# A hybrid block on one Trainium2 core: residual additions moved from GpSimd to VectorE, four down tiles kept open in PSUM, and the last output rows prepared in another order

## The chip, the cores and the metric

The kernel runs on 1 core of one Trainium2 chip. The metric is the device time of one execution in microseconds (us), as the median of several runs. The names of the engines in the rows are PE (TensorE, matrix products; PEld is its weight load), DVE (VectorE), ACT (ScalarE), POOL (GpSimd) and SP (SyncE, which here only issues DMA transfers). A matrix product reads SBUF and writes PSUM, which has 8 banks of 128 x 512 float32 here.

## The reference

The block takes x of 4 batches x 512 tokens x 512 features, runs a gated delta-rule attention on its modulated layer norm, and then a feed-forward part of hidden width 2048:

```
h = _layernorm(x) * (1 + ca) + sa
x = x + ga * attention(h)
h = _layernorm(x) * (1 + cb) + sb
x = x + gb * ffn(h)         # ffn: (silu(h @ Wgate.T) * (h @ Wup.T)) @ Wdown.T
```

The change touches only the last line: the multiplication by the gate gb, the residual addition of x, and the store of the result.

## The kernel before

**The feed-forward part.** It runs as 16 iterations (function `iteration`, L1011). Iterations 0 to 7 treat batches 0 and 1, iterations 8 to 15 batches 2 and 3; each iteration takes one eighth of the hidden width. Every float32 factor is split into a high and a low part, so that a product is three matrix products. An iteration has 22 groups of six matrix products of 512 columns on PE: seven for the gate half (`prod(n, 0..6)` with n = 2 it), seven for the up half (n = 2 it + 1), and between them the eight *down* tiles of the iteration before. The seven products of a half are a Strassen-like scheme for four 128 x 512 blocks; `copy_s` (ACT, out of PSUM) and `cadd` (DVE) combine them. `silu` (ACT), `gated` (DVE), `fh` (ACT) and `fl` (DVE) then make the high and low part (FH, FL) of four blocks of silu(gate) * up.

**A down tile.** `down(it, k)` is one output tile of 128 tokens x 512 features: tile k belongs to the first batch of the two for k = 0 to 3, to the second for k = 4 to 7. PE writes it into one of two PSUM banks, 6 and 7 in turn (`ring_bank`, L890), and waits until DVE has taken the tile before last out of the bank (semaphore `v_y`). DVE adds the tile to its running sum YA[k] in SBUF (L2566).

**The weights.** Each iteration needs gate, up and down weights. For each, SP loads them, POOL forms the sums of the scheme (`w_comb`, L2683 to L2689), ACT makes the high part (`w_high`, one 128 x 1792 copy), and POOL the low part (`w_low_ff`, L2696, seven instructions; `w_high_d`, L2704, four instructions for the down weights). The first product of a half waits for its low part.

**The end of batches 0 and 1.** After the eighth down tile DVE multiplies YA[k] by the gate (`post_0`, into YA[k]). POOL then adds the residual x, which SP has loaded into X1[k] (`add_0`, L2732, eight instructions in iteration 8), and SP stores X1[k] (`store_0`).

**The end of batches 2 and 3.** For the last tiles the work is split: once YA[k] holds the sum of iterations 8 to 14, POOL forms YA[k] * gb + x (`out_pre`, L2739 and L2742; x lies in XO[k]). For `down(15, k)` DVE multiplies the PSUM tile by gb into XO[k] and adds it to YA[k], and SP stores YA[k] (L1458). XO[0] to XO[5] are loaded at iteration 10, XO[6] and XO[7] in iteration 15, since they overlie the gate weights (L1445). XO[0] to XO[3] count on one semaphore (`d_x2`), XO[4] to XO[7] on another (`d_x3`), and `out_pre` waits for all four of its batch:

```
                e.wait_ge(sem(f"d_x{2 + k // 4}"), 80 + 64)
```

In the last iteration `out_pre(0)` stands ahead of the up weights' low part on POOL.

**What sets the order.** One list of steps (`plan`) is written out by hand through calls of `step`. Each engine walks through it, takes the steps it knows and issues its instructions in that order. An instruction that waits for a semaphore holds up all that stand behind it on its engine, SP's DMA issues among them.

Of the kernel before, what the change touches and what calls it, by code (L numbers as in the profile page):

```python
# [53 lines left out]
def build(nc, x, W1, cw, dtb, alog, nw, Wo, cT, wmod, wgu, wdn, cst, out):  # L54
# [956 lines left out]
    def iteration(it):  # L1011
# [111 lines left out]
        cadd(n, 1)  # L1123
        if it and not last:
            down(it - 1, 7)
        if turn:
# [139 lines left out]
    def sync(e):  # L1266
# [21 lines left out]
        for st in plan:  # L1288
# [152 lines left out]
            elif kind == "store_0":  # L1441
                k = st["k"]
                e.wait_ge(sem("p_out"), k + 1)
                e.dma_start(out[k // 4, k % 4 * 128:k % 4 * 128 + 128, :], X1[k][:, :]).then_inc(sem("d_out"), 16)
            elif kind == "load_xo":  # L1445
# [732 lines left out]
    def vector(e):  # L2178
# [16 lines left out]
        for st in plan:  # L2195
# [357 lines left out]
            elif kind == "down":  # L2553
# [3 lines left out]
                if it % 8 == 0:  # L2557
                    if it:
                        e.wait_ge(sem("p_out"), k + 1)
# [4 lines left out]
                elif it < 15:  # L2564
                    e.wait_ge(sem("v_y"), 8 * (it - 1) + k + 1)
                    tt(y, bank(st["bank"]), y, ALU.add).then_inc(sem("v_y"), 1)  # L2566
                else:
                    e.wait_ge(sem("p_out"), 8 + 2 * k + 2)
                    tt(XO[k][:, :], bank(st["bank"]), gbB[k // 4][:, :], ALU.mult).then_inc(sem("v_y"), 1)
                    e.wait_ge(sem("v_y"), 8 * it + k + 1)  # L2570
                    tt(y, y, XO[k][:, :], ALU.add).then_inc(sem("out_x"), 1)
# [7 lines left out]
    def gpsimd(e):  # L2579
# [11 lines left out]
        for st in plan:  # L2591
# [125 lines left out]
            elif kind == "split_h" and st["on"] == "p":  # L2717
# [9 lines left out]
            elif kind == "add_0":
                k = st["k"]
                e.wait_ge(sem("v_om"), k + 1)
                e.wait_ge(sem(f"d_x{k % 2}"), (160, 144)[k % 2])  # L2730
                in_order()
                signal(e.tensor_tensor(X1[k][:, :], YA[k][:, :], X1[k][:, :], ALU.add), "p_out")  # L2732
# [85 lines left out]
```

## Time and profile before

| | |
|---|---|
| Median of 3 runs | 1050.65 us (1048.23 to 1051.37) |
| The profiled execution, its own time | 1049.25 us |
| Span of its trace | 1047.3 us |
| Busy share PE, DVE, ACT, POOL | 95%, 66%, 48%, 53% |

The span runs from the first to the last record of the trace; the execution's own time is 1.95 us longer. All positions below are in us from the start of the span. Iteration 9 begins near 805, iteration 10 near 842 and iteration 15 near 993. In the rows, L1464 is the helper for every matrix product, L1862 that for every ACT instruction, L2180 that for DVE's two-input instructions; POOL's lines tell the steps apart. A row "x30" merges 30 instructions in a row; some matrix-product records are missing from the trace, so counts are not exact. PEclk is the granted clock of TensorE, 1.00 for 2.4 GHz and 0.50 for 1.2 GHz.

### The profile page before, as it was taken

Reading aid. Unit: us, or ns where it says so; the run is one execution under the profiler, and the core shown is the slowest. Engines: PE = TensorE matmul, PEld = TensorE weight load, DVE = VectorE, ACT = ScalarE, POOL = GpSimd, SP = SyncE. Lnnn points to the kernel's source line nnn. Section 1 sums busy time; section 2 is a strip of 40 time slices with the busy share of each in tenths; the row PEclk is TensorE's granted clock in tenths of the full one; section 3 lists DMA queues with packets and bytes.
Section 4 is the critical chain, followed back from the end, with each engine's and each line's share of the span. In section 5 each row is a group of like instructions: output and inputs, shape, how many; then the busy total and the mean of one; then the engine's idle time right before and its main releaser. Section 6 shows DMA issues by size and latency. Waiting matters only on the chain.

```text
span 1047.3 us, 20631 instructions
## 1 busy us (share of the span) xinstructions
PE 996.5 (95%) x7920; PEld 787.9 (75%) x7920; DVE 688.9 (66%) x1044; ACT 501.2 (48%) x891; POOL 555.9 (53%) x597
## 2 busy tenths in 40 slices
PE   7999999999998999999799999999989899999997
PEld 4676777878677888888577777888867688878875
DVE  5977377899964777877763455555577455555447
ACT  3676575345545444554555644334453244434340
POOL 1222530022025554658566555877788866657675
PEclk9999999999998999999999999999999999999999
DMA  6504336938356566656242111111131232111112
GB/s 217 201 11 123 76 82 166 261 101 207 78 127 172 117 136 143 158 122 150 77 141 81 41 42 60 40 61 44 58 118 61 104 121 61 41 61 41 41 41 80
DMA packets 158209, 106.35 MB, mean 102 GB/s; under 512 B 93984, under 2 KB 131104, under 8 KB 157984
## 3 DMA queue, kind: packets, MB, share of 16 engines
q1 hardware_dynamic: 158112, 105.04, 35.9%
q8 instruction: 63, 1.03, 0.4%
q14 instruction: 34, 0.28, 0.1%
HBM read 75.65 MB, written 29.36 MB: 100 GB/s over the span
## 4 chain that ended last, share of the span: by engine, by line
PE 61%; POOL 11%; DVE 11%; ACT 5%; issue 5%; DMA 4%; SPq 2%; POOLq 0%; DVEq 0%; ACTq 0%
PE ps L1464 58%; ACT t L1862 5%; POOL t L2696 4%; DVE t L2180 3%; PE ps L1472 3%; DVE t L2290 2%; DMA scrU<-t 2%; SPq L1325 1%; POOL t L2732 1%; DVE t L2278 1%; PE ps L1703 1%; POOL t L2704 1%; POOL t L2725 1%; DVE t L2390 1%; DVE t L2190 1%
## 5 line engine op out<-in xcount | busy, mean ns | idle before, releaser
L1464 PE MATMUL ps<-t,t 128*128 128x512 f32 (+7 forms) x7100 | 942.5, 326 | 45.1 <-ACT t L1862 13.3
L1464 PEld LDWEIGHTS ps<-t,t 128*128 128x128 f32 (+4 forms) x7100 | 734.6, 160 | 238.2 <-issue 46.3
L2180 DVE TENSOR_TENSOR t<-ps,t 128x512 f32<-128x512 f32 (+2 forms) x336 | 234.3, 707 | 228.6 <-PE ps L1464 156.0
L1862 ACT ACTIVATE t<-t 128x512 fp32r<-128x512 f32 (+11 forms) x433 | 271.3, 650 | 220.8 <-DVE t L2180 95.5
L1862 ACT ACTIVATE t<-ps 128x512 f32<-128x512 f32 (+5 forms) x250 | 138.2, 560 | 244.0 <-PE ps L1464 226.4
L2180 DVE TENSOR_TENSOR t<-t,t 128x512 fp32r<-128x512 f32 (+15 forms) x249 | 208.8, 859 | 44.3 <-ACT t L1862 34.4
L2696 POOL TENSOR_TENSOR t<-t,t 128x256 fp32r<-128x256 f32 x217 | 160.7, 776 | 100.7 <-ACT t L1862 100.1
L1862 ACT ACTIVATE t<-ps,t 128x64 f32<-128x64 f32 (+3 forms) x157 | 74.3, 534 | 25.5 <-PE ps L1472 12.3
L2290 DVE SCALAR_TENSOR_TENSOR t<-ps,t,t 128x511 f32<-128x511 f32 (+2 forms) x108 | 80.2, 747 | 3.4 <-ACT t L1862 0.5
L2704 POOL TENSOR_TENSOR t<-t,t 128x256 fp32r<-128x256 f32 x64 | 63.6, 1024 | 17.3 <-ACT t L1862 15.9
L2627 POOL MEMSET t<- 128x3072 f32 x4 | 10.7, 2668 | 92.5 <-PE ps L1464 70.0
L1472 PE MATMUL ps<-t,t 128*128 128x128 f32 (+1 forms) x340 | 53.7, 288 | 1.6 <-DVE t L2185 1.3
L2671 POOL TENSOR_TENSOR t<-t,t 128x768 fp32r<-128x768 f32 x16 | 29.3, 1830 | 33.5 <-ACT t L1862 33.3
L1472 PEld LDWEIGHTS ps<-t,t 128*128 128x128 f32 (+1 forms) x340 | 39.0, 148 | 10.6 <-issue 5.4
L2608 POOL TENSOR_TENSOR t<-t,t 128x384 fp32r<-128x384 f32 x16 | 14.6, 915 | 52.6 <-PE ps L1464 32.7
L2597 POOL TENSOR_TENSOR t<-t,t 128x512 fp32r<-128x512 f32 x13 | 17.4, 1338 | 46.9 <-ACT t L1862 45.8
L2677 POOL TENSOR_TENSOR t<-t,t 128x512 f32<-128x512 f32 x16 | 21.4, 1337 | 38.1 <-DVE t L2180 37.4
L2683 POOL TENSOR_TENSOR t<-t 128x256 f32<-128x256 f32 x32 | 27.1, 847 | 4.6
L1862 ACT ACTIVATE t<-t,t 128x1 f32<-128x1 f32 (+2 forms) x36 | 13.2, 367 | 33.5 <-DVE t L2192 30.5
L2687 POOL TENSOR_TENSOR t<-t 128x256 f32<-128x256 f32 x32 | 26.4, 825 | 2.5
L2190 DVE BATCH_NORM_STATS2 t<-t 128x6 f32<-128x512 f32 x32 | 21.9, 684 | 8.1 <-DMA t<-in_x 6.4
L2632 POOL MEMSET t<- 128x1536 f32 x1 | 1.4, 1381 | 47.3 <-PE ps L1464 47.3
(60 smaller groups left out, 405.5 us busy)
## 6 DMA issues: line engine op xcount, KB each, us to landing
t<-in_wgu SPq DMA_DIRECT2D x32, 512.0 KB, 3.5
scrU<-t SPq DMA_DIRECT2D x60, 256.0 KB, 3.1
t<-scrU SPq DMA_DIRECT2D x32, 288.0 KB, 4.7
t<-in_wdn SPq DMA_DIRECT2D x32, 256.0 KB, 2.8
t<-scrU SPq DMA_DIRECT2D x32, 192.0 KB, 3.4
t<-in_W SPq DMA_DIRECT2D x19, 256.0 KB, 2.9
t<-in_x SPq DMA_DIRECT2D x16, 256.0 KB, 4.1
t<-in_wmod SPq DMA_DIRECT2D x4, 1024.0 KB, 5.5
```

The lines of the kernel that those rows point to most:

```text
L1464: return e.matmul(o, l, r_, start=start, stop=stop, skip_group_check=True)
L1472: return e.transpose(o, i, idn)
L1862: return e.activation(o, i, f, **kw)
L2180: return e.tensor_tensor(o, a, b, op)
L2190: e.bn_stats(st6[:, slot_, :], src).then_inc(sem(name + "bn"), 1)
L2290: e.scalar_tensor_tensor(yy[:, d + 1:SEQ], p_[:, 0:SEQ - d - 1], cwt[:, j, 2 - d:3 - d], yy[:, d + 1:SEQ], ALU.mult, ALU.add).then_inc(sem ...
L2671: signal(e.tensor_tensor(OZl[:, :, :], OZ[:, :, :], OZh[:, :, :].bitcast(f32), ALU.subtract), "p_ozl")
L2677: signal(e.tensor_tensor(YB[u % 2][:, :], YB[u % 2][:, :], XB[u % 2][:, :], ALU.add), "p_x1")
L2683: signal(e.tensor_tensor(r_[:, 4, :], r_[:, 0, :], r_[:, 3, :], ALU.add), "p_ws")
L2687: signal(e.tensor_tensor(r_[:, 0, :], r_[:, 1, :], r_[:, 0, :], ALU.subtract), "p_ws")
L2696: t = e.tensor_tensor(WGl[m % 3][:, i, :], WR[st["slot"]][:, i, :], WGh[m % 3][:, i, :].bitcast(f32), ALU.subtract)
L2704: t = e.tensor_tensor(WDl[it // 15][:, n, q], WDr[n][:, q], WDh[it // 15][:, n, q].bitcast(f32), ALU.subtract)
```

## The change

1. `add_0` goes from POOL to DVE: k = 0 and 1 in iteration 8 behind `gated(8, 1)`, k = 2, 3 and 4 at the end of iteration 8, and k = 5, 6, 7 in iteration 9, each behind one down tile. The stores move to the end of iteration 9, ahead of the loads of XO[0] to XO[5] in SP's order.
2. In the last iteration the steps of `out_pre` stand in the order 4, 5, (up weights' low part), 0, 1, 2, 3, (down weights' low part), 6, 7.
3. The last four down tiles of iteration 14 (k = 4 to 7) become `down_begun`: they stay open in banks 0, 1, 2 and 6, and `down_last` of iteration 15 accumulates on them, so DVE no longer takes them out. `down_last(0..3)` use banks 7, 4, 5 and 3. `down_begun(4)` stands between products 4 and 5 of the last up half.

```diff
@@ the plan
-        if it == 14:
-            step("out_pre", k=k)
+    HELD = {4: 0, 5: 1, 6: 2, 7: 6}
+    LAST = {0: (7, lambda: ring_free[7]), 1: (4, lambda: [("v_c", 95)]), 2: (5, lambda: [("v_c", 96)]),
+            3: (3, lambda: [("v_gf", 63)])}
+    def down_begun(k):
+        free = ring_free[6] if HELD[k] == 6 else [("v_c", 93), ("a_si", 63)]
+        step("down_begun", k=k, bank=HELD[k], free=free)
@@ iteration, gate half
             if last:
                 w_high(up_m(it), [("prod", 7 * (n - 1) + 7)])
+                out_pre(4)
+                out_pre(5)
+                w_low_ff(up_m(it))
...
             down(it - 1, 0)
+            if last:
+                out_pre(0)
...
+            if last and k < 4:
+                out_pre(k)
+            if it == 9 and k < 4:
+                add_0(k + 4)
@@ iteration, up half
-        if it and not last:
+        if last:
+            down_begun(4)
+        elif it:
             down(it - 1, 7)
...
             if it == 8:
-                for k in range(8):
-                    step("add_0", k=k)
+                add_0(0, 1)
...
         if it == 8:
+            add_0(2, 3, 4)
+        if it == 9:
             for k in range(8):
                 step("store_0", k=k)
@@ the end
-    for k in range(4, 8):
-        down(14, k)
+    for k in range(5, 8):
+        down_begun(k)
+    for k in (6, 7):
+        out_pre(k, [("v_fl", 64)])
     for k in range(8):
-        down(15, k)
+        down_last(k)
@@ DVE
+            elif kind == "down_last":
+                k = st["k"]
+                e.wait_ge(sem("down"), 120 + k + 1)
+                e.wait_ge(sem("p_out"), out_at(k))
+                tt(XO[k][:, :], bank(st["bank"]), gbB[k // 4][:, :], ALU.mult).then_inc(sem("v_y"), 1)
+                e.wait_ge(sem("v_y"), 116 + k + 1)
+                tt(YA[k][:, :], YA[k][:, :], XO[k][:, :], ALU.add).then_inc(sem("out_x"), 1)
+            elif kind == "add_0":
+                k = st["k"]
+                e.wait_ge(sem("v_om"), k + 1)
+                e.wait_ge(sem(f"d_x{k % 2}"), (160, 144)[k % 2])
+                tt(X1[k][:, :], YA[k][:, :], X1[k][:, :], ALU.add).then_inc(sem("v_om"), 1)
@@ POOL, out_pre
-                e.wait_ge(sem("v_y"), 112 + k + 1)
-                if k == 0:
+                e.wait_ge(sem("v_y"), (104 if k > 3 else 112) + k + 1)
+                for tok in st["free"]:
+                    e.wait_ge(*at_least(tok))
+                if k == 4:
                     e.wait_ge(sem("a_grow"), 6)
```

POOL's instructions at the end, before. The tiles t_237 to t_244 are YA[0] to YA[7], t_257 to t_264 are XO[0] to XO[7], t_265 and t_266 the gates; t_185<-t_179 is the low part of the last up weights, t_189 that of the last down weights.

```order
L2739 TENSOR_TENSOR t_237<-t_237,t_265 128x512 [waits p_wl,a_grow,v_y]
L2742 TENSOR_TENSOR t_237<-t_237,t_257 128x512 [waits p_out,d_x2]
L2696 TENSOR_TENSOR t_185<-t_179,t_183 128x256 [waits p_out,a_wh]
L2696 TENSOR_TENSOR t_185<-t_179,t_183 128x256 x6
L2739 TENSOR_TENSOR t_238<-t_238,t_265 128x512 [waits p_wl,v_y]
L2742 TENSOR_TENSOR t_238<-t_238,t_258 128x512 [waits p_out,d_x2]
L2739 TENSOR_TENSOR t_239<-t_239,t_265 128x512 [waits p_out,v_y]
L2742 TENSOR_TENSOR t_239<-t_239,t_259 128x512 [waits p_out,d_x2]
...
L2739 TENSOR_TENSOR t_241<-t_241,t_266 128x512 [waits p_wl,v_y]
L2742 TENSOR_TENSOR t_241<-t_241,t_261 128x512 [waits p_out,d_x3]
```

The same place of the changed kernel:

```order
L2803 TENSOR_TENSOR t_241<-t_241,t_266 128x512 [waits p_wl,a_grow,v_y]
L2806 TENSOR_TENSOR t_241<-t_241,t_261 128x512 [waits p_out,d_x3]
L2803 TENSOR_TENSOR t_242<-t_242,t_266 128x512 [waits p_out,v_y]
L2806 TENSOR_TENSOR t_242<-t_242,t_262 128x512 [waits p_out,d_x3]
L2764 TENSOR_TENSOR t_185<-t_179,t_183 128x256 [waits p_out,a_wh]
L2764 TENSOR_TENSOR t_185<-t_179,t_183 128x256 x6
L2803 TENSOR_TENSOR t_237<-t_237,t_265 128x512 [waits p_wl,v_y]
L2806 TENSOR_TENSOR t_237<-t_237,t_257 128x512 [waits p_out,d_x2]
...
L2803 TENSOR_TENSOR t_243<-t_243,t_266 128x512 [waits p_wl,v_fl,v_y]
L2806 TENSOR_TENSOR t_243<-t_243,t_263 128x512 [waits p_out,d_x3]
```

Two tiles now stand ahead of the low part of the up weights instead of one, and they are tiles 4 and 5, whose addition waits for `d_x3`; tiles 0 to 3 follow it, and tiles 6 and 7 stand behind the down weights.

DVE at the end of iteration 8, before, from `gated(8, 1)` (t_216<-t_232) to `cadd(18, 0)` (t_213<-ps,t_210). The rows t_217<-ps and t_218<-t_234 are `gated(8, 2)` and `gated(8, 3)`, and t_226, t_227, t_228 the `fl` of the last three blocks:

```order
L2180 TENSOR_TENSOR t_216<-t_232,t_216 128x512 [waits v_c,a_si]
L2180 TENSOR_TENSOR t_217<-ps,t_217 128x512 [waits prod,a_si]
L2180 TENSOR_TENSOR t_234<-ps,t_211 128x512 [waits down,prod,a_sp]
L2180 TENSOR_TENSOR t_218<-t_234,t_218 128x512 [waits v_c,a_si]
L2180 TENSOR_TENSOR t_226<-t_216,t_220 128x512 [waits a_fh]
L2180 TENSOR_TENSOR t_227<-t_217,t_221 128x512 [waits a_fh]
L2180 TENSOR_TENSOR t_228<-t_218,t_222 128x512 [waits a_fh]
L2180 TENSOR_TENSOR t_213<-ps,t_210 128x512 [waits v_fl,prod,a_sp]
L2180 TENSOR_TENSOR t_214<-ps,t_212 128x512 [waits v_fl,prod,a_sp]
L2563 COPY t_237<-ps 128x512 [waits p_out,down]
```

The same place of the changed kernel, up to the last `fl`; t_249 to t_253 are X1[0] to X1[4]:

```order
L2241 TENSOR_TENSOR t_216<-t_232,t_216 128x512 [waits v_c,a_si]
L2241 TENSOR_TENSOR t_249<-t_237,t_249 128x512 [waits d_x0,v_om]
L2241 TENSOR_TENSOR t_250<-t_238,t_250 128x512 [waits d_x1,v_om]
L2241 TENSOR_TENSOR t_217<-ps,t_217 128x512 [waits prod,a_si]
L2241 TENSOR_TENSOR t_234<-ps,t_211 128x512 [waits down,prod,a_sp]
L2241 TENSOR_TENSOR t_218<-t_234,t_218 128x512 [waits v_c,a_si]
L2241 TENSOR_TENSOR t_226<-t_216,t_220 128x512 [waits a_fh]
L2241 TENSOR_TENSOR t_227<-t_217,t_221 128x512 [waits a_fh]
L2241 TENSOR_TENSOR t_251<-t_239,t_251 128x512 [waits d_x0,v_om]
L2241 TENSOR_TENSOR t_252<-t_240,t_252 128x512 [waits d_x1,v_om]
L2241 TENSOR_TENSOR t_253<-t_241,t_253 128x512 [waits d_x0,v_om]
L2241 TENSOR_TENSOR t_228<-t_218,t_222 128x512 [waits a_fh]
```

Two additions now stand ahead of `gated(8, 2)` and three ahead of the last `fl` and `cadd(18, 0)`.

PE in the last up half, before: t_201 and t_202 begin products 5 and 6, and t_186<-t_222 a down tile of iteration 14. Only the rows that begin or end a group are shown.

```order
L1464 MATMUL ps<-t_207,t_183 128x512 x2
L1464 MATMUL ps<-t_201,t_183 128x512 [waits a_sp]
...
L1464 MATMUL ps<-t_208,t_183 128x512 x2
L1464 MATMUL ps<-t_202,t_183 128x512 [waits v_c]
...
L1464 MATMUL ps<-t_209,t_183 128x512 x2
L1464 MATMUL ps<-t_186,t_222 128x512 [waits v_fl,v_y]
...
L1464 MATMUL ps<-t_186,t_222 128x512 [waits v_y]
```

The same place of the changed kernel:

```order
L1505 MATMUL ps<-t_207,t_183 128x512 x2
L1505 MATMUL ps<-t_186,t_222 128x512 [waits v_fl,a_si,v_c]
...
L1505 MATMUL ps<-t_187,t_220 128x512
L1505 MATMUL ps<-t_201,t_183 128x512 [waits a_sp]
...
L1505 MATMUL ps<-t_208,t_183 128x512 x2
L1505 MATMUL ps<-t_202,t_183 128x512 [waits v_c]
...
L1505 MATMUL ps<-t_209,t_183 128x512 x2
L1505 MATMUL ps<-t_186,t_222 128x512 [waits a_si,v_c]
```

One down tile has moved ahead of product 5, and these tiles wait for `a_si` and `v_c`, no longer for `v_y`, which DVE counts up when it takes a tile out.

## Rows read from the trace of the kernel before

**Rows 1.** Timeline of PE, 775 to 900: start, us, instructions, [idle before <-releaser]
```profile
...
814.87 11.25 PE L1464 MATMUL ps<-t,t 128*128 128x512 f32 x48 [1.33 <-ACT t L1862]
826.62 3.03 PE L1464 MATMUL ps<-t,t 128*128 128x512 f32 x12 [0.50 <-POOL t L2696]
832.21 68.16 PE L1464 MATMUL ps<-t,t 128*128 128x512 f32 x290 [2.56 <-ACT t L1862]
```

**Rows 2.** Timeline of POOL, 775 to 900
```profile
...
805.85 3.28 POOL L2704 TENSOR_TENSOR t<-t,t 128x256 fp32r<-128x256 f32 x4 [0.43 <-POOL t L2689]
...
821.67 4.90 POOL L2696 TENSOR_TENSOR t<-t,t 128x256 fp32r<-128x256 f32 x7
```

**Rows 3.** Line L2732: ns min/median/max, first and last start
```profile
...
L2732 POOL TENSOR_TENSOR t<-t,t x8: 1287/1298/1529, 809.3 to 820.2; 128x512 f32<-128x512 f32 x8
```

**Rows 4.** Timeline of ACT, 775 to 900
```profile
...
806.00 1.23 ACT L1862 ACTIVATE t<-t 128x512 fp32r<-128x512 f32 x2 [2.55 <-DVE t L2180]
...
814.24 0.58 ACT L1862 ACTIVATE t<-ps 128x512 f32<-128x512 f32 x1
814.72 2.21 ACT L1862 ACTIVATE t<-t 128x1792 fp32r<-128x1792 f32 x2
...
829.98 1.70 ACT L1862 ACTIVATE t<-t 128x1792 fp32r<-128x1792 f32 x1 [10.62 <-POOL t L2689]
```

**Rows 5.** Timeline of DVE, 775 to 900
```profile
...
807.27 5.79 DVE L2180 TENSOR_TENSOR t<-t,t 128x512 f32<-128x512 f32 x4
812.99 0.68 DVE L2180 TENSOR_TENSOR t<-ps,t 128x512 f32<-128x512 f32 x1
...
873.40 3.27 DVE L2180 TENSOR_TENSOR t<-t,t 128x512 f32<-128x512 f32 x4
```

**Rows 6.** Timeline of SP's DMA issues, 775 to 900
```profile
...
845.68 2.76 SPq L1453 DMA_DIRECT2D t<-scrX  x6
856.39 10.89 SPq L1418 DMA_DIRECT2D t<-in_wgu  x2
```

**Rows 7.** Stretches: us, busy of the five, PEclk, DMA share, GB/s
```profile
...
832.20:837.00 4.80, 4.79 (x14) 3.83 (x15) 2.61 (x3) 1.11 (x2) 4.80 (x7) 0.64 0.01 3
...
1010.80:1012.50 1.70, 0.00 (x1) 0.00 (x0) 0.69 (x1) 0.00 (x0) 1.66 (x3) 1.00 0.00 0
```

**Rows 8.** Timeline of PE, 985 to the end
```profile
...
1012.51 7.10 PE L1464 MATMUL ps<-t,t 128*128 128x512 f32 x30 [1.71 <-POOL t L2696]
1020.29 5.78 PE L1464 MATMUL ps<-t,t 128*128 128x512 f32 x24 [0.69 <-ACT t L1862]
1027.86 15.30 PE L1464 MATMUL ps<-t,t 128*128 128x512 f32 x60 [1.79 <-DVE t L2180]
```

**Rows 9.** Timeline of POOL, 985 to the end
```profile
...
994.29 3.85 POOL L2704 TENSOR_TENSOR t<-t,t 128x256 fp32r<-128x256 f32 x4 [0.30 <-ACT t L1862]
1004.72 1.29 POOL L2739 TENSOR_TENSOR t<-t,t 128x512 f32<-128x512 f32 x1 [6.59 <-DVE t L2180]
...
1007.60 4.86 POOL L2696 TENSOR_TENSOR t<-t,t 128x256 fp32r<-128x256 f32 x7
...
1038.74 1.55 POOL L2742 TENSOR_TENSOR t<-t,t 128x512 f32<-128x512 f32 x1
```

**Rows 10.** Timeline of SP's DMA issues, 985 to the end
```profile
...
1006.71 0.80 SPq L1453 DMA_DIRECT2D t<-scrX  x2
```

**Rows 11.** DMA issues, 985 to the end: count, KB each, median us to landing
```profile
...
t<-scrX SPq DMA_DIRECT2D x2, 256.0 KB, 2.8
```

**Rows 12.** Timeline of DVE, 985 to the end
```profile
...
1009.48 0.69 DVE L2180 TENSOR_TENSOR t<-ps,t 128x512 f32<-128x512 f32 x1 [0.68 <-PE ps L1464]
1010.84 0.69 DVE L2180 TENSOR_TENSOR t<-ps,t 128x512 f32<-128x512 f32 x1 [0.67 <-PE ps L1464]
...
1038.08 1.06 DVE L2180 TENSOR_TENSOR t<-t,t 128x512 f32<-128x512 f32 x1
...
1040.76 0.68 DVE L2180 TENSOR_TENSOR t<-ps,t 128x512 f32<-128x512 f32 x1
```

More of the change, by code:

```diff
@@ L901, in down, with out_pre, out_at, add_0 @@
             step("post_0", k=k)
-        if it == 14:
-            step("out_pre", k=k)
+    out_order = []
+    def out_pre(k, free=()):
+        step("out_pre", k=k, free=list(free))
+        out_order.append(k)
+    def out_at(k):
+        return 2 * out_order.index(k) + 2
+    def add_0(*ks):
+        for k in ks:
+            step("add_0", k=k)
+    HELD = {4: 0, 5: 1, 6: 2, 7: 6}
[4 more added lines that the diff above has]
+        step("down_begun", k=k, bank=HELD[k], free=free)
+        tick("down")
+    def down_last(k):
+        i, free = (HELD[k], lambda: []) if k in HELD else LAST[k]
+        step("down_last", k=k, bank=i, free=free(), begun=k in HELD)
+        tick("down")
+        tick("v_y")
     def gate_row(b):
@@ L1066, in iteration @@
             step("silu", it=it, t=1)
-            w_load_next(it, w_low_ff(up_m(it)))
+            if not last:
+                w_load_next(it, w_low_ff(up_m(it)))
             prod(n, 5)
@@ L1442, in sync @@
                 k = st["k"]
-                e.wait_ge(sem("p_out"), k + 1)
+                e.wait_ge(sem("v_om"), 8 + k + 1)
                 e.dma_start(out[k // 4, k % 4 * 128:k % 4 * 128 + 128, :], X1[k][:, :]).then_inc(sem("d_out"), 16)
@@ L1454, in sync @@
                         sem(f"d_x{2 + k // 4}"), 16)
-            elif kind == "down" and st["it"] == 15:
+            elif kind == "down_last":
                 k = st["k"]
@@ L1857, in tensor @@
                     t = mm3(bank(st["bank"]), FH[f][:, tk], FL[f][:, tk], WDh[it // 15][:, jj, :], WDl[it // 15][:, jj, :], jj == 0, jj == 1)
+                t.then_inc(sem("down"), 1)
+            elif kind in ("down_begun", "down_last"):
+                k = st["k"]
+                b, s = k // 4, k % 4
+                tk = slice(s * 128, (s + 1) * 128)
+                ahead = kind == "down_begun"
+                it = 14 if ahead else 15
+                for tok in st["free"]:
+                    e.wait_ge(*at_least(tok))
+                if ahead and k == 4:
+                    e.wait_ge(sem("v_fl"), 60)
+                elif not ahead and s == 0:
+                    e.wait_ge(sem("v_fl"), 64 if b else 63)
+                if not ahead and k == 0:
+                    e.wait_ge(*at_least(w_low_at[47]))
+                opens = ahead or not st["begun"]
+                for jj, t_ in enumerate(((0, 2), (3, 1))[b]):
+                    f = f_of(it, t_)
+                    t = mm3(bank(st["bank"]), FH[f][:, tk], FL[f][:, tk], WDh[it // 15][:, jj, :], WDl[it // 15][:, jj, :],
+                            opens and jj == 0, not ahead and jj == 1)
                 t.then_inc(sem("down"), 1)
@@ L2558, in vector @@
                     if it:
-                        e.wait_ge(sem("p_out"), k + 1)
+                        e.wait_ge(sem("v_om"), 8 + k + 1)
                     else:
@@ L2563, in vector @@
                     e.tensor_copy(y, bank(st["bank"])).then_inc(sem("v_y"), 1)
-                elif it < 15:
+                else:
                     e.wait_ge(sem("v_y"), 8 * (it - 1) + k + 1)
                     tt(y, bank(st["bank"]), y, ALU.add).then_inc(sem("v_y"), 1)
[L2567 to L2571, printed above, removed]
+            elif kind == "down_last":
+                k = st["k"]
[5 more added lines that the diff above has]
+            elif kind == "add_0":
+                k = st["k"]
+                e.wait_ge(sem("v_om"), k + 1)
+                e.wait_ge(sem(f"d_x{k % 2}"), (160, 144)[k % 2])
+                tt(X1[k][:, :], YA[k][:, :], X1[k][:, :], ALU.add).then_inc(sem("v_om"), 1)
             elif kind == "post_0":
@@ L2726, in gpsimd @@
                 signal(t, "p_hs")
[L2727 to L2732, printed above, removed]
             elif kind == "out_pre":
                 k = st["k"]
-                e.wait_ge(sem("v_y"), 112 + k + 1)
-                if k == 0:
+                e.wait_ge(sem("v_y"), (104 if k > 3 else 112) + k + 1)
+                for tok in st["free"]:
+                    e.wait_ge(*at_least(tok))
+                if k == 4:
                     e.wait_ge(sem("a_grow"), 6)
```

## The prediction

> **What bounds the kernel now.** I read the timelines of the five engines beside each other at the two places that the change touches, and at each place asked which wait ends last.
>
> From 775 to 900, PE's timeline shows three waits in iteration 9: 1.33 us before 814.87, for ACT; 0.50 us before 826.62, for POOL's low part of the up weights; and 2.56 us before 832.21, for ACT again. After that it runs to 900 without a gap [rows 1]. POOL's timeline explains the second: the low part of the down weights ends at 809.13, and the low part of the up weights, seven instructions, only starts at 821.67 and ends at 826.57 [rows 2]. The eight additions lie between, 1.29 to 1.53 us each [rows 3], 12.5 us in all with their gaps. The third follows from the same backlog: the weight copy at 829.98, 1.70 us long, came when POOL's sums were done, and a PSUM copy that PE wants stands behind it on ACT; ACT had idled 10.62 us for it [rows 4]. The first wait has to do with DVE. Four of its SBUF instructions took 5.79 us beside POOL's additions, and `cadd(18, 0)` came only at 812.99; the same four take 3.27 us in iteration 10 [rows 5]. `silu(9, 0)` waits for that `cadd`, the copy at 814.24 stands behind it on ACT [rows 4], and PE waits for the copy. The stores and loads behind the additions are in SP's order [rows 6].
>
> The waits have a second price, the clock. After the 2.56 us gap the granted clock was 0.64 over the next 4.80 us, so it had fallen to 1.2 GHz for most of them; that is 4.80 x 0.36 = 1.7 us of work lost. Over the 1.70 us gap at 1010.80 it stayed at 1.00, 2.4 GHz [rows 7].
>
> At the end, PE waits 1.71 us for POOL before 1012.51, 0.69 us for ACT before 1020.29, and 1.79 us for DVE before 1027.86; the last ten groups take 15.30 us [rows 8]. POOL idles 6.59 us before its first `out_pre` at 1004.72, which then stands ahead of the low part at 1007.60 [rows 9]. SP issues the loads of XO[6] and XO[7] at 1006.71, when the gate products are through [rows 10]; such a load lands in 2.8 us [rows 11]. A down tile takes PE 1.36 us, as DVE's evictions at 1009.48 and 1010.84 show [rows 12].
>
> **The change part by part: iterations 8 and 9.** Without the additions POOL's low part can start when ACT's weight copy is done: 814.72 + 1.70 [rows 4] = 816.4 instead of 821.67, 5.2 us earlier, and what hangs on it comes earlier by as much. PE wanted it 0.50 us earlier, and the copy behind it 2.56 us earlier, so both waits go, with the slow clock behind them: 0.50 + 2.56 + 1.7 = 4.8 us.
>
> Against that, DVE gets eight instructions. Two stand ahead of `gated(8, 2)`. They run beside POOL's down weights, so I take 1.06 us each, which an addition takes beside POOL [rows 12]: 2.1 us. ACT's `fh(8, 2)`, the second instruction at 806.00 [rows 4], waits for it, and the copy that PE needs behind it, so a wait of about 2 us appears earlier. The next three run while POOL now idles: 0.69 us each, 2.1 us. The four at 807.27 shrink from 5.79 to 4 x 0.7 = 2.8 us. So `cadd(18, 0)` comes 2.1 + 2.1 - 3.0 = 1.2 us later; as SBUF instructions overlap by up to 0.1 us each, I take 0.8. The three in iteration 9 each stand between two evictions: 0.69 + 1.06 = 1.75 us against PE's 1.36, three times 0.4, less the 0.67 that DVE has free, is 0.5 us. The five additions cost nothing further while ACT and the second bank hide them. The gain here is 4.8 - 0.8 - 0.5 = 3.5 us. Bounds: 4.8 if all is hidden; 0.7 by the first rival below.
>
> The page SBUF: State Buffer of the Trainium skill (two separate sides) says that a DVE instruction with two SBUF inputs and a GpSimd instruction that reads SBUF exclude each other for a whole instruction. By that rule each of the first two additions could wait out one low-part instruction, 3.28 / 4 = 0.82 us, and last 1.5 us instead of 1.06, which would make the gain 2.6 us. That additions took 1.45 us each beside POOL's 512-wide ones and 1.06 at the end speaks for a wait of less than a whole instruction on average.
>
> SP: eight stores now lie ahead of the loads at 845.68, at 2.76 / 6 = 0.46 us each 3.7 us, then a landing of some 3 us, for which the loads wait, then their 2.8 us. That is 9.5 us of the 10.7 until the next weight load at 856.39 [rows 6]. Hidden; if not, 2 us of lateness meet some 10 us before the weights are used.
>
> **The end.** Here a new wait arises. POOL's second instruction for tile 4 waits for `d_x3`, and that count holds all of XO[4] to XO[7]. XO[6] and XO[7] are issued at 1006.71; the second leaves 0.4 us later and lands 2.8 us later, at 1009.9. In before, POOL had other work until then. Now the multiplication of tile 4 fits into POOL's idle time after 998.1, and then POOL stands still, with the up weights' low part queued behind it and PE waiting for that. Then come three instructions of 1.44 us (1.29 and the gap), 4.3 us, and 4.86 us of low part: 1019.1. PE starts the up half 6.6 us later than at 1012.51.
>
> PE then loses fewer waits: 0.69 (a down tile stands in it), 1.79 (no eviction is needed), 15.30 - 10 x 1.36 = 1.7 and 5.78 - 4 x 1.36 = 0.3 us [rows 8]: 4.5 us. The count of groups is unchanged. POOL's next work, eight instructions of tiles 0 to 3 at about 1.5 us and 3 to 3.9 us of down weights [rows 9], ends by 1035.1. PE comes to the first last tile at 1019.1 + 7.1 + 6 x 1.36 = 1034.4, or 1036.1 with the slow clock: no wait then, 0.7 us if the clock held.
>
> PE idles from 1010.8 to 1019.1, 8.3 us, three times the gap after which the clock fell [rows 7]. I charge the same 1.7 us. The page TensorE: Matmul & The Clock Gate of the Trainium skill (Part 1) says that an idle array is granted half rate; its rule would not change this term.
>
> DVE's last part: tiles 6 and 7 on POOL run until about 1042, and beside POOL a tile costs DVE 1.70 us, against 1.33 later and PE's 1.36. Some three tiles times 0.34 less a little regained is 0.8 us at the end. The stretch from DVE's last instruction to the end of the span is unchanged.
>
> End: 6.6 - 4.5 + 1.7 + 0.8 = +4.6 us. Bounds: +2.8 with neither clock nor lag; +7 with the slow clock twice as long and a later landing.
>
> **Sum.** +4.6 - 3.5 = +1.1 us. It is made against the profiled execution: 1047.3 becomes 1048.4 us of span, and its own time of 1049.25 becomes 1050.35. The median of the runs is 1.4 us above that execution, so 1051.7 us.
>
> **The rivals.** *Slower:* the gap in iteration 8 slows the clock. It grows from 1.33 us to more than 2; 1.71 did not cost the clock and 2.56 did. If the three additions ahead of the last `fl` also take 1.06 us, 1.1 us more, the gap passes 2.5 us, and the clock takes 1.7 us. The gain is 3.5 - 2.8 = 0.7, the time 1050.65 + 3.9 = 1054.5 us. For it speaks how near the numbers lie; against it, that the wait falls into two pieces and that POOL idles there. It decides from 2.5 us in one piece on. *Slower at the end:* the 8.3 us gap leaves a longer stretch of slow clock, or the loads land later, by 2 us together: 1053.7 us. *Faster:* POOL is not held by `d_x3`, because the loads are in time. Then PE's 1.71 us go too, and the end gains 1.7 + 4.5 - 0.8 = 5.4 us, with the 3.5 before: 1041.8 us. Against it stands that the loads wait for products that end at 1006.7, 8 us after POOL is ready. *The stores on SP* delay the weights: against it the margin above; a lateness of 3 us on PE would make 1054.7 us.
>
> **How the numbers follow.** Forecast 0.60, first rival 0.20, second 0.08, the faster one 0.07, the stores 0.05. A measurement of this kernel tells about 0.3%, 3.15 us, from no change: 1047.5 to 1053.8 us. The forecast's own spread is 1048.3 (4.8 gained, 2.8 - 0.3 lost) to 1054. A sixth of it (0.10) passes 1053.8 and a fifteenth (0.04) falls under 1047.5; of the first rival 0.15, of the second 0.04 and of the stores 0.04 pass 1053.8. That makes 0.11 faster with the third rival, 0.33 slower, and 0.56 within. The range for 8 in 10 reaches from 1048.0 to 1056.0 us, to the slower cases and without the faster one.
>
> **What would show it.** Right: in iteration 9 no PE wait for POOL, the clock at 1.00 from 826 to 840, PE waits of 2 to 2.5 us in all between 805 and 817; at the end a POOL wait of about 10 us for a DMA, PE idle about 8 us for the up weights' low part, a clock of 0.5 after it, and no PE wait for DVE in the last 14 us. Wrong: POOL's instruction of tile 4 before 1004; a PE gap of over 2.5 us near 810 to 816 with the clock down; the up weights of iteration 11 late because of SP.

## The result, and the profile after

| | before | changed |
|---|---|---|
| median of 20 runs | 1048.8 us (1046.3 to 1053.0) | 1051.2 us (1047.5 to 1056.9) |
| ratio | | 1.0024, 95% interval 1.0013 to 1.0035 |
| span of the profiled execution | 1047.3 us | 1048.3 us |

The changed kernel is 0.24% slower, 2.4 us by the medians. The spans differ by only 1.0 us, because the changed execution was already 1.2 us ahead before any changed code: PE's restart in iteration 8 lies at 780.29 instead of 781.46. So I count from places inside the program, and not from the start of the span.

PE's timeline of the changed kernel from 770 to 870. The waits of 0.50 and 2.56 us of [rows 1] are gone; one of 2.40 us has come at 808.90, where product 2 of half 18 waits for ACT's copy. After it PE runs without a gap.

```profile
...
795.21 11.29 PE L1505 MATMUL ps<-t,t 128*128 128x512 f32 x48 [0.45 <-ACT t L1923]
808.90 61.45 PE L1505 MATMUL ps<-t,t 128*128 128x512 f32 x261 [2.40 <-ACT t L1923]
```

POOL, same stretch: behind the down weights it now idles 8.71 us, and the low part of the up weights follows ACT's copy, where [rows 2] had it at 821.67 behind the additions.

```profile
...
804.66 3.71 POOL L2772 TENSOR_TENSOR t<-t,t 128x256 fp32r<-128x256 f32 x4 [0.43 <-POOL t L2757]
817.08 5.37 POOL L2764 TENSOR_TENSOR t<-t,t 128x256 fp32r<-128x256 f32 x7 [8.71 <-ACT t L1923]
```

ACT: the two `fh` that stood together at 806.00 [rows 4] are now 2.28 us apart, since the second waits for `gated(8, 2)`; the copy for PE stands behind it. The weight copy at 826.70 no longer holds anybody.

```profile
...
804.82 0.64 ACT L1923 ACTIVATE t<-t 128x512 fp32r<-128x512 f32 x1 [2.54 <-DVE t L2241]
807.73 0.63 ACT L1923 ACTIVATE t<-t 128x512 fp32r<-128x512 f32 x1 [2.28 <-DVE t L2241]
808.27 0.58 ACT L1923 ACTIVATE t<-ps 128x512 f32<-128x512 f32 x1
...
826.70 1.70 ACT L1923 ACTIVATE t<-t 128x1792 fp32r<-128x1792 f32 x1 [6.32 <-POOL t L2757]
```

DVE: four instructions with the first two additions, 4.62 us; then seven in 4.30 us, with three additions, while POOL idles, against 5.79 us for four in [rows 5]; `cadd(18, 0)` at 812.62. Of the three additions between evictions the first takes 0.88 us, the other two 0.68 each.

```profile
...
802.48 4.62 DVE L2241 TENSOR_TENSOR t<-t,t 128x512 f32<-128x512 f32 x4
...
808.40 4.30 DVE L2241 TENSOR_TENSOR t<-t,t 128x512 f32<-128x512 f32 x7
812.62 0.68 DVE L2241 TENSOR_TENSOR t<-ps,t 128x512 f32<-128x512 f32 x1
...
820.97 0.88 DVE L2241 TENSOR_TENSOR t<-t,t 128x512 f32<-128x512 f32 x1
...
822.37 0.68 DVE L2241 TENSOR_TENSOR t<-t,t 128x512 f32<-128x512 f32 x1
```

SP: the stores, the loads and the next weight load in [rows 6]'s place. The weights are issued at 853.63, right behind the loads, and 847.25 + 4.91 = 852.16 is when POOL freed their buffer: 1.5 us late, which shows on no engine.

```profile
...
842.76 5.43 SPq L1485 DMA_DIRECT2D out<-t  x8
850.88 2.71 SPq L1494 DMA_DIRECT2D t<-scrX  x6
853.63 9.44 SPq L1459 DMA_DIRECT2D t<-in_wgu  x2
```

The end. PE's timeline: one wait of 8.32 us for POOL's low part, and then no other, where [rows 8] has 1.71, 0.69 and 1.79.

```profile
...
1014.92 29.02 PE L1505 MATMUL ps<-t,t 128*128 128x512 f32 x114 [8.32 <-POOL t L2764]
```

POOL, against [rows 9]: the multiplication of tile 4 at 994.10, then 10.21 us of waiting for a DMA, two more instructions of tile 5, and only then the low part of the up weights (L2764) that PE waits for. The down weights' low part (L2772) ends at 1030.1, before PE needs it.

```profile
...
994.10 1.53 POOL L2803 TENSOR_TENSOR t<-t,t 128x512 f32<-128x512 f32 x1 [0.17 <-POOL t L2772]
1005.84 1.27 POOL L2806 TENSOR_TENSOR t<-t,t 128x512 f32<-128x512 f32 x1 [10.21 <-DMA t<-scrX]
...
1008.66 1.26 POOL L2806 TENSOR_TENSOR t<-t,t 128x512 f32<-128x512 f32 x1
1010.06 4.80 POOL L2764 TENSOR_TENSOR t<-t,t 128x256 fp32r<-128x256 f32 x7
...
1026.98 3.10 POOL L2772 TENSOR_TENSOR t<-t,t 128x256 fp32r<-128x256 f32 x4
...
1037.14 1.56 POOL L2806 TENSOR_TENSOR t<-t,t 128x512 f32<-128x512 f32 x1
```

SP issues the loads that POOL waits for at 1002.51 ([rows 10]: 1006.71, the same step):

```profile
...
1002.51 0.80 SPq L1494 DMA_DIRECT2D t<-scrX  x2
```

The granted clock (the columns are those of [rows 7]) behind both waits: 0.50 for 3 us behind the first. In the second it fell while PE still waited, and from PE's restart at 1014.92 on it stayed at 0.50 until some 0.4 us after 1020.

```profile
...
808.90:811.90 3.00, 3.00 (x7) 2.42 (x8) 3.00 (x6) 0.67 (x2) 0.00 (x0) 0.50 0.51 175
811.90:814.90 3.00, 3.00 (x14) 2.41 (x14) 1.41 (x3) 1.28 (x3) 0.00 (x0) 0.96 0.00 0
1010.00:1018.00 8.00, 3.08 (x7) 2.49 (x8) 0.00 (x0) 0.11 (x1) 7.51 (x10) 0.51 0.01 2
1018.00:1020.00 2.00, 2.00 (x6) 1.54 (x5) 0.00 (x0) 0.48 (x1) 1.86 (x2) 0.50 0.00 0
1020.00:1022.00 2.00, 2.00 (x9) 1.59 (x9) 1.40 (x2) 0.11 (x1) 1.83 (x2) 0.91 0.00 0
```

DVE's last instructions: a tile costs 1.70 us while POOL works on tiles 6 and 7, and 1.33 later; the last tile starts 0.54 us after PE's end at 1043.94, against 0.25 us in the kernel before.

```profile
...
1038.19 1.07 DVE L2241 TENSOR_TENSOR t<-t,t 128x512 f32<-128x512 f32 x1
...
1039.89 0.69 DVE L2241 TENSOR_TENSOR t<-t,t 128x512 f32<-128x512 f32 x1
...
1044.48 0.68 DVE L2241 TENSOR_TENSOR t<-ps,t 128x512 f32<-128x512 f32 x1
```

### The profile page after: what moved, and what is told of

It reads as the page before. It is cut to its first block, busy times and chain, and to the rows that moved or that the text cites. A ratio compares the mean times of both kernels' runs of the same rounds, so it can differ in the third digit from the quotient of the medians.

```text
span 1048.3 us, 20624 instructions
## 1 busy us (share of the span) xinstructions
PE 994.5 (95%) x7920; PEld 788.7 (75%) x7920; DVE 690.9 (66%) x1048; ACT 502.3 (48%) x891; POOL 546.9 (52%) x589
## 4 chain that ended last, share of the span: by engine, by line
PE 66%; DVE 10%; POOL 7%; ACT 5%; issue 4%; DMA 4%; SPq 3%; DVEq 0%; POOLq 0%; ACTq 0%
PE ps L1505 62%; ACT t L1923 4%; PE ps L1513 3%; DVE t L2241 3%; DVE t L2351 2%; POOL t L2764 2%; DMA scrU<-t 2%; SPq L1366 1%; DVE t L2339 1%; PE ps L1744 1%; POOL t L2793 1%; DVE t L2451 1%; DMA scrA<-t 1%; DVE t L2251 1%; DVE t L2462 1%
## 5 line engine op out<-in xcount | busy, mean ns | idle before, releaser
L1505 PE MATMUL ps<-t,t 128*128 128x512 f32 (+7 forms) x7100 | 941.0, 325 | 47.8 <-ACT t L1923 11.3
L2241 DVE TENSOR_TENSOR t<-ps,t 128x512 f32<-128x512 f32 (+2 forms) x332 | 231.1, 706 | 232.2 <-PE ps L1505 169.9
L2241 DVE TENSOR_TENSOR t<-t,t 128x512 fp32r<-128x512 f32 (+14 forms) x257 | 214.5, 856 | 43.3 <-ACT t L1923 33.1
L2764 POOL TENSOR_TENSOR t<-t,t 128x256 fp32r<-128x256 f32 x217 | 161.3, 778 | 107.5 <-ACT t L1923 107.1
L2772 POOL TENSOR_TENSOR t<-t,t 128x256 fp32r<-128x256 f32 x64 | 64.2, 1033 | 17.3 <-ACT t L1923 15.9
L2665 POOL TENSOR_TENSOR t<-t,t 128x512 fp32r<-128x512 f32 x13 | 17.4, 1340 | 46.8 <-ACT t L1923 45.7
L2751 POOL TENSOR_TENSOR t<-t 128x256 f32<-128x256 f32 x32 | 27.7, 864 | 4.6
L2755 POOL TENSOR_TENSOR t<-t 128x256 f32<-128x256 f32 x32 | 26.1, 817 | 2.5
L2757 POOL TENSOR_TENSOR t<-t 128x256 f32<-128x256 f32 x32 | 25.2, 788 | 2.5
```

The source lines that it names most:

```text
L1505: return e.matmul(o, l, r_, start=start, stop=stop, skip_group_check=True)
L2241: return e.tensor_tensor(o, a, b, op)
L2751: signal(e.tensor_tensor(r_[:, 4, :], r_[:, 0, :], r_[:, 3, :], ALU.add), "p_ws")
L2755: signal(e.tensor_tensor(r_[:, 0, :], r_[:, 1, :], r_[:, 0, :], ALU.subtract), "p_ws")
L2757: signal(e.tensor_tensor(r_[:, 6, :], r_[:, 2, :], r_[:, 5, :], ALU.subtract), "p_ws")
L2764: t = e.tensor_tensor(WGl[m % 3][:, i, :], WR[st["slot"]][:, i, :], WGh[m % 3][:, i, :].bitcast(f32), ALU.subtract)
```

## The experiments

All eight were timed beside the kernel before, e1 to e4 together and e5 to e8 together, and the changed kernel at another time. So a difference to the changed kernel is best read from the two ratios to the kernel before; by them e1 is 9.2 us below it, by the medians 10.0. As executions of one kernel spread by several us, I also read two stretches of each profiled execution: *A* from PE's restart in iteration 8 (781.46 in the kernel before) to SP's issue of XO[6] and XO[7] (1006.71), which holds all that the additions and stores can do; and *B* from there to the end of the span.

| kernel | median us | ratio to before (95%) | A | B |
|---|---|---|---|---|
| before | | 1 | 225.3 | 40.6 |
| changed | 1051.2 | 1.0024 (1.0013 to 1.0035) | 222.2 | 45.8 |
| e1, own count | 1041.2 | 0.9936 (0.9921 to 0.9952) | 222.4 | 36.1 |
| e2, additions only | 1046.6 | 0.9980 (0.9959 to 1.0000) | 220.9 | 41.6 |
| e3, end only | 1054.2 | 1.0065 (1.0047 to 1.0082) | 223.6 | 46.0 |
| e4, filled gap | 1050.3 | 1.0016 (1.0002 to 1.0030) | 222.3 | 45.4 |
| e5, both mended | 1037.8 | 0.9906 (0.9882 to 0.9930) | 219.3 | 36.0 |
| e6, held tiles alone | 1047.3 | 0.9983 (0.9971 to 0.9996) | 223.6 | 38.8 |
| e7, weights first | 1046.1 | 0.9960 (0.9946 to 0.9974) | 220.8 | 41.5 |
| e8, additions later | 1051.0 | 1.0015 (1.0002 to 1.0029) | 222.4 | 45.7 |

The kernel before had medians of 1048.6 us beside e1 to e4 and 1049.0 us beside e5 to e8.

**e1: is it the shared count?** The loads of XO[6] and XO[7] count on another semaphore, which only the first loads of the kernel use:

```diff
-                        sem(f"d_x{2 + k // 4}"), 16)
+                        sem("d_x4" if k > 5 else f"d_x{2 + k // 4}"), 16)
...
-                e.wait_ge(sem(f"d_x{2 + k // 4}"), 80 + 64)
+                e.wait_ge(*((sem("d_x4"), 80) if k > 5 else (sem(f"d_x{2 + k // 4}"), 80 + (32 if k > 3 else 64))))
```

> The changed kernel with one edit: the loads of XO[6] and XO[7] count on a semaphore of their own, and POOL's additions of tiles 4 and 5 wait only for XO[4] and XO[5], loaded in iteration 10. Theory (the shared count holds POOL, and the slow clock follows from PE's wait): POOL's addition of tile 4 comes right behind its multiplication, the low part of the up weights ends before PE has done its down tiles, PE starts the up half without a wait 8.3 us earlier, the clock stays at 1.00, which gives 2.7 us more; 11 us less than the changed kernel, about 1040 us. Rival (two tiles ahead of the weights are too much work for POOL, whatever they wait for): a PE wait of 1.5 us or more for the low part stays, and the time is 1043 us or more.

9 to 10 us less than the changed kernel, and B is 9.7 us shorter. PE's timeline has no wait at the up half any more; the one before the last eight tiles is 0.39 us:

```profile
...
810.32 213.05 PE L1505 MATMUL ps<-t,t 128*128 128x512 f32 x916 [2.44 <-ACT t L1923]
1023.76 11.30 PE L1505 MATMUL ps<-t,t 128*128 128x512 f32 x48 [0.39 <-DVE t L2241]
```

POOL does both tiles back to back, in what was idle time, and the low part (L2764) ends at 1006.9, 1.3 us before PE is done with its down tiles:

```profile
...
995.48 1.53 POOL L2803 TENSOR_TENSOR t<-t,t 128x512 f32<-128x512 f32 x1 [0.17 <-POOL t L2772]
997.15 1.57 POOL L2806 TENSOR_TENSOR t<-t,t 128x512 f32<-128x512 f32 x1
...
1002.01 4.92 POOL L2764 TENSOR_TENSOR t<-t,t 128x256 fp32r<-128x256 f32 x7
```

The rival falls: the two tiles fit. The expectation of 8.3 + 2.7 = 11 us was 1.3 too large for B; the 0.39 us are one part of that, and VectorE's last instruction ends 2.65 us after PE, against 1.95 in the changed kernel.

**e2: the additions alone.** The kernel before with part 1 of the change only.

> The kernel before with only the residual additions on VectorE and the stores at the end of iteration 9; the end as before. Theory: PE reaches the end of its first gate product of iteration 10 some 3.0 us earlier than in the kernel before, counted from its restart in iteration 8, and the time is 3 us less, 1045.8 us; a PE wait of 2.4 us for ACT with a clock below 1.00 behind it shows near 808. Rival (the wait and the clock take back all): 1048.8 us, within 0.5 us of before.

2.1 us less by the ratio, with no change just at the end of the interval, so the time does not decide between the two. The wait of 2.44 us is there, but this time the clock did not fall behind it, so A is 4.4 us shorter, not 3.0:

```profile
...
808.19:811.19 3.00, 3.00 (x13) 2.50 (x14) 3.00 (x6) 1.23 (x2) 0.00 (x0) 1.00 0.61 175
```

Instead it fell behind the 1.79 us wait at the end, which the kernel before has too ([rows 8]) without this loss; that makes B 1.0 us longer, although nothing was changed there:

```profile
...
1021.60:1025.00 3.40, 3.40 (x9) 2.68 (x10) 1.23 (x2) 0.00 (x0) 3.10 (x3) 0.56 0.00 0
```

**e3: the end alone.** The changed kernel with `add_0` on POOL in iteration 8 and the stores there.

> The changed kernel with the additions back on GpSimd in iteration 8 and the stores there: only the end is changed. Theory: the stretch from SP's loads of XO[6] and XO[7] to the end of the span is 45.8 us against 40.6 in the kernel before, and the time is 5.2 us more, 1054 us. Rival (the two places interact, since the end gets its clock or its order from earlier work): the time is within 2 us of before.

5.6 us more by the medians, and B is 46.0, as the theory has it; the rival falls. The two parts add up as well as such runs can tell: -1.9 and +5.6 us by the medians against +2.4 for both, with intervals of some 2 us on each side of the single ones. In A the clock held behind the 2.56 us wait that in the kernel before had cost it:

```profile
...
832.39:834.39 2.00, 2.00 (x9) 1.66 (x10) 1.41 (x2) 0.31 (x1) 2.00 (x3) 1.00 0.00 0
```

**e4: the clock by itself.** 32 matrix products in the gap, behind the third down tile, for whose result nobody asks:

```diff
             step("load_xo", ks=(6, 7))
+            step("keep")
...
+            elif kind == "keep":
+                e.wait_ge(sem("v_c"), 93)
+                e.wait_ge(sem("a_si"), 63)
+                for _ in range(32):
+                    mm(bank(0), FH[0][:, 0:128], WDh[0][:, 0, :], True, True)
```

> The changed kernel with 32 additional matrix products (their result goes to bank 0 and is overwritten) behind the third down tile of iteration 15, ahead of the product that waits for the up weights; they take some 7 us of PE's 8.3 us wait. It isolates the clock. Theory (the rest of the loss at the end is the clock): the wait for POOL ends at the same place, the clock is 1.00 behind it, and the time is 2.7 us less than the changed kernel, 1048.5 us. Rival (PE's groups behind the wait are slow for another reason, the semaphores or PSUM): the time stays at 1051.2 us although the clock is 1.00.

The clock stays at 1.00 and the time hardly moves: 0.8 us less than the changed kernel by the ratios, within their intervals. That is the rival's time, but not for its reason, since PE's groups behind the wait do get faster. PE comes to the last eight tiles 28.0 us after SP's issue, against 30.5 in the changed kernel (1043.94 - 8 x 1.36 - 1002.51), and loses most of these 2.5 us to a wait that did not exist in the changed kernel: 1.61 us for the low part of the down weights.

```profile
...
1017.82 15.38 PE L1506 MATMUL ps<-t,t 128*128 128x512 f32 x66 [1.24 <-POOL t L2770]
1034.81 11.32 PE L1506 MATMUL ps<-t,t 128*128 128x512 f32 x48 [1.61 <-POOL t L2778]
```

```profile
...
1008.57 1.29 POOL L2812 TENSOR_TENSOR t<-t,t 128x512 f32<-128x512 f32 x1 [10.22 <-DMA t<-scrX]
...
1028.78 1.30 POOL L2812 TENSOR_TENSOR t<-t,t 128x512 f32<-128x512 f32 x1
1030.22 4.45 POOL L2778 TENSOR_TENSOR t<-t,t 128x256 fp32r<-128x256 f32 x4
```

In the changed kernel POOL ends the down weights' low part 27.6 us after SP's issue, here 29.4 us after it (1034.67 - 1005.23), and had it kept to 27.6, PE, which comes at 28.0, would not have waited. 1.35 of these 1.9 us lie in the four instructions of the low part, 4.45 us against 3.10. They run beside four `fl` of DVE, which come 2.4 us earlier, counted from the issue, because PE is faster, and which take 4.12 us instead of 2.82:

```profile
...
1029.96 4.12 DVE L2247 TENSOR_TENSOR t<-t,t 128x512 f32<-128x512 f32 x4
```

So a faster PE makes DVE and POOL meet, and that costs most of what it gains; removing the slow clock alone is worth 0.4 us in B.

**e5: the additions off ACT's path as well.** e1, and the additions 0 and 1 behind `cadd(18, 0)`, 2 and 3 behind the first down tile, 4 to 7 behind down tiles 1 to 4 of iteration 9.

```diff
             cadd(n, 0)
+            if it == 9:
+                add_0(0, 1)
...
             down(it - 1, 0)
+            if it == 9:
+                add_0(2, 3)
...
-            if it == 9 and k < 4:
-                add_0(k + 4)
+            if it == 9 and k < 5:
+                add_0(k + 3)
...
             if it == 8:
-                add_0(0, 1)
+                pass
...
-        if it == 8:
-            add_0(2, 3, 4)
```

> The version with XO[6] and XO[7] counted apart, and the eight additions all in iteration 9: 0 and 1 behind the first cadd, 2 and 3 behind the first down tile, 4 to 7 behind down tiles 1 to 4. Theory (two additions ahead of gated(8, 2) hold ACT's copy and so PE, 2.4 us and the clock after it): the wait near 808 goes, no other of over 0.5 us comes, and the time is 2.4 to 3.7 us less than that version, 1038.2 us. Rival (VectorE has no room for eight additions in iteration 9 either): a wait of the same size appears between 812 and 828, and the time stays at 1041 us.

As expected: 1037.8 us, 0.94% under the kernel before, and the fastest of all. The wait at 808 and the clock behind it are gone; 0.39 us at 825.34 has come:

```profile
...
794.07 30.87 PE L1507 MATMUL ps<-t,t 128*128 128x512 f32 x132 [0.45 <-ACT t L1925]
825.34 192.37 PE L1507 MATMUL ps<-t,t 128*128 128x512 f32 x832 [0.39 <-ACT t L1925]
1018.10 11.34 PE L1507 MATMUL ps<-t,t 128*128 128x512 f32 x48 [0.39 <-DVE t L2243]
```

**e6: the held tiles alone.** The kernel before with `down_begun` and `down_last`, and `out_pre` in its old order 0 to 7.

> The kernel before with only the down tiles 4 to 7 of iteration 14 kept open and the banks and place of the last tiles as in the changed kernel; the additions on GpSimd in iteration 8 and the order of out_pre 0 to 7 as before. Theory (held tiles are worth 4.5 us less a lag of VectorE): the 1.71 us wait for the up weights stays, those of 0.69 and 1.79 us go, the last groups run dense, VectorE lags by up to 2 us beside POOL's last tiles; the stretch from the loads of XO[6] and XO[7] to the end is 38 us against 40.6 before, the time 1046.2 us. Rival (a held tile gains nothing, the end is bound by POOL and VectorE): 40 us or more, 1048.5 us.

1.8 us less by the ratio, between the theories. The 1.71 us wait stays, and those of 0.69 and 1.79 us became one of 1.01:

```profile
...
1010.62 15.39 PE L1498 MATMUL ps<-t,t 128*128 128x512 f32 x66 [1.71 <-POOL t L2752]
1027.03 11.33 PE L1498 MATMUL ps<-t,t 128*128 128x512 f32 x48 [1.01 <-issue]
```

The row names no releaser. By the kernel these products need the `fl`, the third of which ends at 1026.93, 0.1 us before PE goes on. DVE makes the `fl` beside POOL's tiles 4 and 5: four instructions in 5.85 us. In the changed kernel the same four take 2.82 us, since POOL only begins with tile 6 when the last `fl` is done.

```profile
...
1022.78 5.85 DVE L2234 TENSOR_TENSOR t<-t,t 128x512 f32<-128x512 f32 x4
```

```profile
...
1029.62 2.82 DVE L2241 TENSOR_TENSOR t<-t,t 128x512 f32<-128x512 f32 x4
```

**e7: the weights ahead of the two tiles.** The changed kernel with `w_low_ff(up_m(it))` ahead of `out_pre(4)` and `out_pre(5)`.

> The changed kernel with the low part of the up weights ahead of tiles 4 and 5 on POOL; the shared count stays. Theory: PE starts the up half without a wait, but POOL still stands still until the loads land, and then has eleven instructions of tiles 4, 5, 0 to 3 ahead of the down weights' low part; PE waits some 4 us for it before the last eight tiles; the stretch from the loads to the end is 40 us, the time 1045.4 us. Rival (only the place of the up weights matters): no wait of over 1 us, 36 us as in the version with a count of its own, 1041.2 us.

0.4% under the kernel before, 1046.1 us where 1045.4 was expected. PE starts the up half at once, and then waits 5.05 us for L2772, 1 us more than I had expected; its last eight tiles take 13.27 us instead of the 11.3 of e1, since the clock fell in that wait and was 0.50 for 4.3 us behind it. That makes B 41.5 instead of 40. A is 1.4 us shorter than in the changed kernel with the same code there: behind its 2.41 us wait the clock stayed at 1.00. The rival falls:

```profile
...
1026.83 13.27 PE L1505 MATMUL ps<-t,t 128*128 128x512 f32 x48 [5.05 <-POOL t L2772]
```

```profile
...
1003.04 1.30 POOL L2803 TENSOR_TENSOR t<-t,t 128x512 f32<-128x512 f32 x1 [0.17 <-POOL t L2764]
1005.90 1.29 POOL L2806 TENSOR_TENSOR t<-t,t 128x512 f32<-128x512 f32 x1 [1.56 <-DMA t<-scrX]
...
1023.21 3.48 POOL L2772 TENSOR_TENSOR t<-t,t 128x256 fp32r<-128x256 f32 x4
```

**e8: the first two additions behind the fl.** The changed kernel with `add_0(0, 1, 2, 3, 4)` at the end of iteration 8.

> The changed kernel with additions 0 and 1 moved behind the second and third fl of iteration 8, to the other three; five additions now stand ahead of the last fl and cadd(18, 0). Theory (the chain through cadd(18, 0), silu and ACT's copy is what ends last, and the additions lengthen it wherever they stand ahead of it): the wait near 808 goes and one of about 2.3 us comes before product 5 near 814; the time is that of the changed kernel, 1051.2 us. Rival (only the copy that PE waits for at 808 matters): no such wait, 2.4 us less, 1048.8 us.

The time is that of the changed kernel, and the rival falls. The wait at 808 has gone, and one of 2.13 us has come before product 5, at 816.14, again with the slow clock behind it:

```profile
...
796.85 17.16 PE L1505 MATMUL ps<-t,t 128*128 128x512 f32 x72 [0.46 <-ACT t L1923]
816.14 192.27 PE L1505 MATMUL ps<-t,t 128*128 128x512 f32 x826 [2.13 <-ACT t L1923]
```

```profile
...
816.14:819.14 3.00, 3.00 (x8) 2.38 (x9) 1.27 (x2) 2.34 (x3) 1.39 (x3) 0.55 0.00 0
```

## Why the prediction was right, and where its sizes were off

*Iterations 8 and 9.* Right: the two waits behind POOL's backlog go, SP's stores stay hidden, and `cadd(18, 0)` comes 0.8 us later, counted from product 2 of half 17 (796.41 before, 795.21 after): 16.58 us before, 17.41 after. e8 shows that it is this chain, and not only the `fh`, that ends last. I took 3.5 us of gain and A gives 3.0.

The term that was mis-sized is the clock, "1.7 us": I counted it as won, but it fell again behind the new wait, 3 us at 0.50, 1.6 us lost. I had that as the first rival, from 2.5 us in one piece on, and had put against it that the wait would fall into two pieces; it came as one of 2.40, and that was enough; my sign of being wrong, over 2.5 us with the clock down, stood 0.1 us away. The bound of 2.5 us was no bound: the clock fell behind 2.13 us in e8 and behind 1.79 us in e2, and held behind 2.56 us in e3 and e6. So the 1.7 us that I read in one execution of the kernel before are not in every execution; where the clock held on both sides, A goes from 223.6 (e3, e6) to 220.9 (e2), 2.7 us.

Other errors made up for most of the 1.6 us. The additions between evictions, which I had charged 0.5 us, cost nothing: they took 0.88, 0.68 and 0.68 us, where I had taken 1.06 each. PE's wait grew by 1.07 us (1.33 to 2.40) and not by 0.8. And 0.9 us more was gained than these terms explain: 3.5 - 1.6 + 0.5 - 0.3 + 0.9 = 3.0. When e3 and e2, whose clock held in both, are matched matrix product by matrix product, PE loses 1.5, 0.6 and 2.8 us at the three waits of [rows 1], 0.5 us more than the rows print in their brackets; where the rest lies is open.

The 1.45 us "beside POOL's 512-wide ones" in the prediction is a mean over two cases and over no addition: of the four instructions at 807.27 the first two ran beside the low part and took 1.25 and 1.22 us, the other two beside POOL's additions and took 1.78 and 1.77. The first pair was the one to take for the two additions ahead of `gated(8, 2)`, which run beside the low part as well: they took 1.24 and 1.23 us, more than my 1.06. By the rule of the page SBUF: State Buffer in the Trainium skill (two separate sides), one instruction waits out the other's, and I had worked out 1.5 us from it. The trace agrees that both sides pay: alone the additions take 0.68 us, and two of POOL's four low-part instructions took 1.17 and 1.19 us beside them instead of 0.74. But the additions waited some 0.55 us each, less than a whole instruction of POOL.

*The new wait.* Right to the place and nearly to the tenth. From SP's issue: POOL's addition of tile 4 starts 3.33 us later (I had 3.2), PE starts the up half 12.41 us later against 5.80, 6.6 us more (6.6), after 8.32 us of idleness (8.3). e1 shows the cause, since it changes only what is counted.

*What PE recovers.* From its start to its end PE takes 29.02 us against 30.65. The clock cost 3.08 / 2 + 2.00 / 2 + 2.00 x 0.09 = 2.7 us of that, so the recovery is 4.3 us (4.5). The term "the same 1.7 us" was too small: the half rate held for some 5.4 us from the restart. VectorE's lag is 0.3 us (0.8), since tiles 6 and 7 were done at 1038.7 and not at 1042. 6.6 - 4.3 + 2.7 + 0.3 = 5.3, and B gives 5.2 where I had 4.6.

*The sum.* 5.2 - 3.0 = +2.2 us by the two stretches, +2.4 by the medians, +1.1 forecast: the direction and the mechanism were right, the size was half of what came. The absolute 1051.7 us lies closer to 1051.2 than that deserves: it started from the median of three runs, 1050.65, and twenty gave 1048.8.

*What I did not foresee* is that the clock's price at the end would be nearly void. I had written that without it PE would wait 0.7 us for the down weights, and charged it in full; e4 shows a wait of 1.61 us, since DVE's `fl` then come beside POOL's low part and lengthen it, and with it nearly the time of the changed kernel.

## What to carry to other kernels

When work is moved ahead, look up what each of its waits counts, not only what it needs: a semaphore that is shared by early and late transfers makes the early ones as late as the last, and all that stands behind on that engine with them. In this kernel that one count was worth 9 to 10 us of 1050, and hid that the rest of the change was good. A wait removed on one chain is worth only what the next chain leaves (e4, e7), and an instruction taken from a full engine costs where the new engine's order feeds a third one (e8); put it where that engine idles between two dependent steps (e5).

## What the runs showed of the hardware that I had not expected

The same wait of PE does not always cost the clock. Behind 2.56 us the granted clock fell to 0.50 for over 3 us in the kernel before and stayed at 1.00 in e3 and e6; behind 2.40 to 2.44 us it fell in the changed kernel, e1 and e4 and stayed in e2 and e7. Shorter waits cost it too: 2.13 us in e8, and 1.79 us in e2, where the kernel before kept 1.00 behind the same 1.79 us. So in these traces the length of a wait between 1.8 and 2.6 us does not tell whether the clock falls. Between such executions of like code A differs by 1.3 to 1.7 us (222.2 and 220.9; 225.3 and 223.6). Behind the wait of 8.3 us it was at 0.50 in the changed kernel for some 5.4 us, longer than behind the short ones.

Part of the spread of single runs goes with the clock, but not most: over the 48 executions of the kernel before that were timed beside the experiments, those with a lower granted clock tend to be longer, with a correlation of -0.45, which is a fifth of the variance.

Where VectorE and GpSimd both work on two SBUF tiles at a time, both pay. A 128 x 512 instruction of VectorE took 0.68 us alone, 1.22 to 1.25 beside GpSimd's 256-wide low part of the down weights, and 1.05 to 1.78 beside its 512-wide instructions, which themselves took some 1.55 instead of 1.30 us.
